# Setup and counting tables in one stage; rescaling and u's first half moved in attention

## The chip, the cores and the metric

The kernel runs on one core of a Trainium2 chip, as one program. Its time is the device time of an execution in microseconds. Engines: PE is TensorE's matmul, PEld its weight load, DVE is VectorE, ACT ScalarE, POOL GpSimd, SP SyncE, which here only issues DMAs. Each engine works through its own queue in order; semaphores order the engines among each other.

## The reference

A graph of N = 3125 nodes with 64 features and E = 103,125 edges, sorted by destination. Four layers, each of the form x = layernorm(x + layer(x)):

```
L0: mean of x[src] over the edges of a dst, two 64x64 products, batch norm, relu
L1: h = x * rsqrt(out_deg[src]); sum over edges * rsqrt(in_deg[dst]); @ W + b
L2: attention over edges. Per edge e, with S = 9 harmonics sh, hidden MLPs wk, wv:
    k[e] = wk[e] * sum_{d,s} x[dst_e,d] * sh[e,s] * Cqk[d,s,:]     (v alike with Cv)
    attn[e,h] = <q[src_e,h], k[e,h]>; softmax over the edges of a node; sum of v * alpha
    @ W_out + x @ W_self, batch norm
L3: messages relu(concat(x[s], x[t]) @ W_msg + b), mean per node, update product, relu
```

The edge list holds each random edge in both directions and one loop per node; the kernel gathers the rows of one end of an edge with an indirect DMA and reaches those of the other by windows of 128 nodes, since dst is sorted.

## The kernel before

Edges are cut into 808 tiles of 128, four tiles to a group of 512 edges: 202 groups. The stages run one behind the other; each is a block of code per engine, and between two blocks all engines meet at a barrier.

**setup** (L98 to L243 of the kernel before). SP (L157) and ACT (L167) issue the loads of all constants and of the edge and node tables, alternately, on one semaphore `loaded`. DVE waits for all of them (ahead of L204), converts dst to float (L204), splits the weight tables Cqk and Cv in a high and a low part (L211 to L216), makes two scaled edge lists (L218 to L221), which SP stores, and `dst_local` and `node_of_part` (L230, L232) from a matmul (L241). POOL fills constants and the identity.

**group_tables** (L253 to L427). The counting stage needs to know which tiles touch which window of 16 nodes. SP loads `tile_last` (L291); POOL writes four iotas (L295 to L301). DVE goes through a chain of some 30 short dependent steps (L351 to L399), with two small matmuls in it (L314, L319), and gets the tile numbers `tile_i`. POOL then gathers the 12 blocks of edge rows with indirect DMAs (L306). DVE waits for all twelve (ahead of L402), computes `lo_f` and `off` from them (to L423), PE transposes both, 12 + 12 (L325, L327), slot by slot, and ACT (L336) and DVE (L427) copy them to `lo_tab` and `key_tab`.

**count_and_sum** (L456 on). DVE first clears the sums (L485), sets the ones in `pieces` (L486) and splits the node rows in three bf16 parts (`split_rows`, L433 to L439). Then for each group of tiles it makes one-hots (L494, L496), PE multiplies them to counts (L538), ACT copies the counts out (L564). Layers 0 and 1 follow.

**attention_loop**. A pipeline over groups g, written out by hand as `body(g)` on each engine; in body g the first work on group g+1 stands beside the last work on group g-1. The order on DVE in one body: z parts 0 and 1 of g+1 (L1547), vx of g-1 (L1576), then in turn low parts 0, 1, 2 (L1553) and z parts 2, 3, 4, low part 3 (L1553), low part 4 (L1556, on partitions 64 to 127 only), u = b_k * wk (L1606), u = b_q * u (L1609), vw (L1612), the pick table of g+2 (L1534), the two scans run (L1583) and top (L1586) that give the running maximum per node, ex (L1591, L1593). ACT makes the high part of each z (L1282), which the low part needs. PE sums u over the heads (L1497), then picks q, sums the previous group by node (L1504, L1507), transposes the gathered rows of the next group (L1423), which ACT copies to `xt` (L1259), and multiplies the z parts with Cqk and Cv (L1450 to L1456).

POOL keeps the sums of all nodes, `acc_den`. Per group it rescales the first column by the factor with which the running maximum moved (L1355), adds the group's four tiles at their windows (L1360), and gathers the rows of a later group, four indirect DMAs (L1341). The rescaling and the adds are one function `add(g)`; it waits for the sums of g and for all five low parts of g+3 (`low_ready`), which DVE makes in body g+2:

```
with pool.Fori(0, G // 2 - 3) as n:
    add(2 * n + 1, 1)
    gather(2 * n + 6, n + 3, 0, False)
    add(2 * n + 2, 0)
    gather(2 * n + 7, n + 3, 1, False)
```

DVE writes `ex` of group g only after the rescaling of g-2 has read it (`added`). The message stage and layer 3 follow attention.

## Time and profile before

| | us |
|---|---|
| median of 3 runs | 5087.5 (5077.75 to 5090.65) |
| profiled execution, its own time | 5084.4 |
| its span, first to last instruction | 5082.7 |
| PE busy | 4378.5 (86%) |
| DVE busy | 4062.3 (80%) |
| ACT busy | 2575.0 (51%) |
| POOL busy | 2381.0 (47%) |

| stretch, us | stage |
|---|---|
| 0 to 34 | setup |
| 34 to 90 | group_tables |
| 90 to 106 | clearing and row split at the head of count_and_sum |
| 106 to 700 | counting |
| 1047 to 3883 | attention |
| from there to 5083 | layer 2's end, messages, layer 3 |

A timeline line gives the start in us, the duration in us, the engine, the line of the kernel, the operation, output <- inputs, and in brackets how long the engine had been idle before it and what released it. SPq, ACTq are DMA issues. Groups of instructions give the number (x), total and mean duration. The granted clock is a fraction of the full one.

### The profile page before, as it was taken

The numbers are of one execution on the slowest core, as the hardware profiler recorded it, in microseconds if no ns is written. First come the engines' busy times: TensorE is split into PE (matmuls) and PEld (weight loads), VectorE is DVE, ScalarE is ACT, GpSimd is POOL, SyncE is SP. The second block draws the span as 40 slices with busy tenths as digits, with TensorE's granted clock in tenths as the row PEclk, the third lists the DMA queues.
The fourth block names the chain that finished last, engine by engine and source line by source line (L and its number), as shares of the span: only waits on it lengthen the run. The fifth ranks groups of instructions, "written<-read, shape, count | busy, mean of one in ns | idle before, by whom it ended". The sixth has DMA issues, their size and how long they took to land. (4 is left out here: it accounts for less than half of the span.)

```text
span 5082.7 us, 93633 instructions
## 1 busy us (share of the span) xinstructions
PE 4378.5 (86%) x21874; PEld 3160.3 (62%) x21874; DVE 4062.3 (80%) x9260; ACT 2575.0 (51%) x5924; POOL 2381.0 (47%) x2660
## 2 busy tenths in 40 slices
PE   1787877879999999999999999999998677777777
PEld 0222343457777777777777777777777566666665
DVE  5999965469999999999999999999994455555554
ACT  0777750047777777777777777777773100000000
POOL 1000000035555555555555555555552477777774
PEclk9999988879999999999999999999997555555555
DMA  2112115378888887888788888788882344444442
GB/s 57 76 76 98 79 51 232 145 165 180 180 180 180 178 180 179 181 179 181 178 179 182 180 180 181 177 181 180 179 181 52 76 100 103 101 103 103 102 103 63
DMA packets 576585, 719.35 MB, mean 142 GB/s; under 512 B 204519, under 2 KB 338727, under 8 KB 572583
## 3 DMA queue, kind: packets, MB, share of 16 engines
q1 hardware_dynamic: 517910, 634.65, 50.5%
q0 software_dynamic: 52288, 81.11, 8.1%
q10 hardware_dynamic: 6288, 2.48, 0.2%
q8 instruction: 38, 0.62, 0.1%
q14 instruction: 61, 0.49, 0.0%
HBM read 663.58 MB, written 54.36 MB: 141 GB/s over the span
## 5 line engine op out<-in xcount | busy, mean ns | idle before, releaser
L1341 POOL DMA_INDIRECT attn_rows<-x_twice,attn_idx x808 | 960.0, 1188 | 237.5 <-issue 203.9
L1696 POOL DMA_INDIRECT msg_rows<-a_rows,msg_idx x808 | 779.0, 964 | 370.2 <-issue 243.6
L1547 DVE TENSOR_TENSOR attn_z<-attn_xt,attn_sh 128x512 f32<-128x512 f32 x1010 | 681.8, 691 | 67.7 <-ACT attn_xt L1259 42.9
L1282 ACT CAST attn_z_hi<-attn_z 128x512 fp32r<-128x512 f32 x1010 | 606.8, 623 | 204.0 <-DVE attn_z L1547 197.6
L1360 POOL TENSOR_TENSOR acc_den<-acc_den,attn_sums 128x256 f32 x808 | 582.7, 721 | 188.7 <-POOL acc_den L1360 151.9
L1734 PE MATMUL msg_at_dst<-msg_bwin,msg_pick 128*128 128x64 f32 x1616 | 397.6, 428 | 271.1 <-DVE msg_pick L1760 218.7
L1734 PEld LDWEIGHTS msg_at_dst<-msg_bwin,msg_pick 128*128 128x128 f32 x1616 | 359.8, 328 | 351.3 <-DVE msg_pick L1760 263.1
L1674 ACT ACTIVATE msg_msg<-msg_pre 128x256 f32<-128x256 f32 x202 | 84.2, 417 | 941.8 <-DVE msg_pre L1775 937.7
L1553 DVE TENSOR_TENSOR attn_z_lo<-attn_z,attn_z_hi 128x512 fp32r<-128x512 f32 x808 | 555.0, 687 | 1.0 <-ACT attn_z_hi L1282 0.8
L1362 POOL MEMSET acc_den<- 128x6656 f32 x1 | 5.6, 5645 | 980.2 <-POOLq L90 980.2
L538 PE MATMUL count_bank<-count_key_hot,count_lo_hot 128*128 128x400 bf16 x1395 | 330.7, 348 | 135.9 <-DVE count_key_hot L496 132.1
L496 DVE TENSOR_SCALAR count_key_hot<-key_iota,key_tab 128x400 bf16<-128x400 f16 x1395 | 429.6, 308 | 0.1
L1355 POOL TENSOR_TENSOR acc_den<-acc_den,attn_ex 128x2 f32 x202 | 38.9, 193 | 822.7 <-DVE attn_z_hi L1556 803.1
L1775 DVE TENSOR_TENSOR msg_pre<-msg_rows,msg_at_dst 128x256 f32<-128x256 f32 x202 | 85.1, 421 | 416.4 <-DMA msg_rows<-a_rows,msg_idx 416.4
L1745 PE MATMUL msg_sums<-msg_onehot,msg_msg 128*64 128x128 f32 x1616 | 397.8, 428 | 2.7 <-ACT msg_msg L1674 2.7
L538 PEld LDWEIGHTS count_bank<-count_key_hot,count_lo_hot 128*128 128x128 bf16 x1395 | 102.9, 100 | 386.9 <-DVE count_key_hot L496 327.2
L1450 PE MATMUL attn_b_v<-attn_z_hi,L_Cv_hi 128*128 128x512 f32 x808 | 340.0, 421 | 0.0
L1450 PE MATMUL attn_b_k<-attn_z_hi,L_Cqk_hi 128*128 128x512 f32 x808 | 335.4, 415 | 0.0
L1745 PEld LDWEIGHTS msg_sums<-msg_onehot,msg_msg 128*64 128x64 f32 x1616 | 317.1, 225 | 26.7 <-ACT msg_msg L1674 3.1
L494 DVE TENSOR_SCALAR count_lo_hot<-lo_iota,lo_tab 128x128 bf16<-128x128 f16 x1395 | 332.8, 239 | 0.0
L1452 PE MATMUL attn_b_k<-attn_z_lo,L_Cqk_hi 128*128 128x512 f32 x808 | 318.4, 394 | 0.0
L1451 PE MATMUL attn_b_v<-attn_z_hi,L_Cv_lo 128*128 128x512 f32 x808 | 317.2, 393 | 0.0
(294 smaller groups left out, 10985.6 us busy)
## 6 DMA issues: line engine op xcount, KB each, us to landing
attn_sh<-in_edge_sh SPq DMA_DIRECT2D x404, 640.0 KB
attn_dst<-dst_scaled SPq DMA_DIRECT2D x202, 256.0 KB
attn_qwin<-q_rows SPq DMA_DIRECT2D x808, 64.0 KB
attn_mask<-dst_step SPq DMA_DIRECT2D x202, 256.0 KB, 3.5
msg_dst<-dst_scaled SPq DMA_DIRECT2D x202, 256.0 KB, 3.2
counts<-chunk SPq DMA_DIRECT2D x15, 3100.0 KB, 9.7
chunk_late<-counts SPq DMA_DIRECT2D x15, 3100.0 KB, 10.3
attn_feat<-in_edge_feat SPq DMA_DIRECT2D x404, 64.0 KB
```

What stands on the lines that cost most here:

```text
L494: nc.vector.tensor_scalar(lo_hot[g % RING][:, s, :], sb["lo_iota"][:], sb["lo_tab"][:, s, g:g + 1], None, ALU.is_equal)
L496: ts = nc.vector.tensor_scalar(key_hot[g % RING][:, s, :], sb["key_iota"][:], sb["key_tab"][:, s, g:g + 1], None, ALU.is_equal)
L538: mm = nc.tensor.matmul(bank[g % 4][:, 0:KEYS], lo_hot[g % RING][:, s, :], key_hot[g % RING][:, s, :], start=(s == 0), stop=(s == SLOTS - 1))
L1282: nc.scalar.copy(z_hi[p][:, c, :], z[:, c % 2, :]).then_inc(high_sb, 1)
L1341: pool.indirect_dma_start(rows[p][:, t, :], None, dram["x_twice"], bass.IndirectOffsetOnAxis(ap=idx[p][:, t:t + 1], axis=0)).then_inc(rows ...
L1360: pool.tensor_tensor(window, window, sums[p][:, :, t, :], ALU.add).then_inc(added, 1)
L1450: nc.tensor.matmul(bank[:], hi[:, c, :], z_hi[p][:, c, :], start=(c == 0), stop=False)
L1547: dve.tensor_tensor(z[:, c % 2, :], xt[p][:], sh[p][:, c, :], ALU.mult).then_inc(z_ready, 1)
L1553: dve.tensor_tensor(z_lo[p][:, c, :], z[:, c % 2, :], z_hi[p][:, c, :].bitcast(F32), ALU.subtract).then_inc(low_ready, 1)
L1696: pool.indirect_dma_start(rows[p][:, t, :], None, dram["a_rows"], bass.IndirectOffsetOnAxis(ap=idx[p][:, t:t + 1], axis=0)).then_inc(rows_ ...
L1734: mm = nc.tensor.matmul(at_dst[p][:, t * D:(t + 1) * D], pick[p][:, t, :], bwin[p][:, t, :], start=True, stop=True)
L1745: mm = nc.tensor.matmul(sums[p][0:D, t, :], msg[p][:, t, :], onehot[p][:, t, :], start=True, stop=True)
```

## The change

setup and group_tables become one block, in place of the latter. `tile_last` is the first load on SP, with a semaphore of its own; the node rows are the first load on ACT, with their own too, and leave the common list, which shifts the alternation of the loads behind them. DVE goes through the tables' chain first; while POOL gathers, it splits the node rows (taken from count_and_sum) and then does the old setup's work; then it waits for the gathers. POOL writes the tables' four iotas first and, behind the constants, clears the sums and sets the ones of `pieces`. PE transposes the lo parts as soon as they are there, the key parts when the old setup's tables have been read out of the same PSUM banks. In attention POOL's rescaling becomes `fade(g)`, issued after `add(g-1)` and ahead of the next gathers; it waits for ex of g and for the top scan of g+1. On DVE low part 4 of the next group moves behind u's first product.

The diff, cut to its core (the chain of L348 to L399 is the same code in the new place):

```diff
         ph = Phase(nc, ctx, "setup")
         loaded = ph.sem("loaded")
         iota_done = ph.sem("iota_done")
+        x_in = ph.sem("x_in")
+        piece_step, pieces_done, cleared = (ph.sem(n) for n in ("piece_step", "pieces_done", "cleared"))
...
+        rest = ph.sb("rest", [P, HB, D])
...
         def _(sp):
+            sp.dma_start(last[:], dram["tile_last"].rearrange("(p k) -> p k", p=P)).then_inc(last_in, 16)
             for to, frm in loads[0::2]:
...
+            act.dma_start(sb["x_rows"][:], dram["x"][0:HB * P, :].rearrange("(h l) d -> l h d", l=P)).then_inc(x_in, 16)
             for to, frm in loads[1::2]:
...
+            act.wait_ge(turned, 1)
+            nc.scalar.copy(sb["win_base"][0:1, :], turn_ps[0:1, 0:GK * P]).then_inc(copied, 1)
+            act.wait_ge(turned, 2)
+            for s in range(SLOTS):
+                nc.scalar.copy(sb["lo_tab"][:, s, :], lo_ps[s][:].rearrange("p k g -> p (k g)")).then_inc(copied, 1)
             act.wait_ge(padded, 64)
...
+            pool.iota(win_iota[:], [[1, NWIN]], base=0, channel_multiplier=0,
+                      allow_small_or_imprecise_dtypes=True).then_inc(ranged, 1)
...
+            pool.memset(sb["acc"][:], 0.0).then_inc(cleared, 1)
+            pool.memset(sb["pieces"][:, :, 2 * D:3 * D], 1.0).then_inc(cleared, 1)
+            pool.wait_ge(sized, 1)
+            for k in range(GK):
+                for s in range(SLOTS):
+                    pool.indirect_dma_start(
+                        edges[:, k, s, :], None, dram["edge_table"],
+                        bass.IndirectOffsetOnAxis(ap=tile_i[:, k, s:s + 1], axis=0)).then_inc(rows_in, 16)
...
+            pe.wait_ge(placed, 1)
+            for k in range(GK):
+                mm = nc.tensor.matmul(turn_ps[0:1, k * P:(k + 1) * P], win_base[:, k:k + 1], sb["ident"][:],
+                                      start=True, stop=True)
+            mm.then_inc(turned, 1)
+            key_flat = [key_ps[k][:].rearrange("p k g -> p (k g)") for k in range(2)]
+            pe.wait_ge(step, 2)
+            pe.wait_ge(dst_float, 1)
+            half = T // 2
+            for k in range(2):
+                mm = nc.tensor.matmul(key_flat[k][:, 0:half], first_row[:], dst_f[:, k * half:(k + 1) * half],
+                                      start=True, stop=True)
+            mm.then_inc(base_bcast, 1)
+            pe.wait_ge(keyed, 1)
+            for s in range(SLOTS):
+                for k in range(GK):
+                    mm = nc.tensor.transpose(lo_ps[s][:, k, :], lo_f[:, k, s, :], sb["ident"][:])
+            mm.then_inc(turned, 1)
+            pe.wait_ge(keyed, 2)
+            pe.wait_ge(tables_done, 5)
+            for s in range(SLOTS):
+                for k in range(GK):
+                    mm = nc.tensor.transpose(key_ps[s][:, k, :], off[:, k, s, :], sb["ident"][:])
+                mm.then_inc(turned, 1)

...
+            dve.tensor_scalar(tile_i[:], tile[:], float(T - 1), None, ALU.min).then_inc(sized, 1)
+            n = 22 + SLOTS
+            dve.wait_ge(x_in, 16)
+            dve.wait_ge(cleared, 2)
+            split_rows(dve, piece_step, sb["pieces"], sb["x_rows"][:], rest[:], 0, pieces_done)
             dve.wait_ge(loaded, 16 * len(loads))
             dve.tensor_copy(dst_f[:], sb["dst_i"][:]).then_inc(dst_float, 1)
...
-                dve.tensor_tensor(sb["dst_local"][:, cols], dst_f[:, cols], base_ps[:, k, 0:half],
+                dve.tensor_tensor(sb["dst_local"][:, cols], dst_f[:, cols], key_flat[k][:, 0:half],
...
-            dve.memset(sb["acc"][:], 0.0).then_inc(cleared, 1)
-            dve.memset(sb["pieces"][:, :, 2 * D:3 * D], 1.0).then_inc(cleared, 1)
-            split_rows(dve, piece_step, sb["pieces"], sb["x_rows"][:], rest[:], 0, pieces_done)
-            dve.wait_ge(cleared, 2)
-
...
-            pe.wait_ge(pieces_done, 1)
...
-            def add(g, p):
-
-                bases = window_bases(nc, mybir.EngineType.Pool, sb, TG * g)
+            def fade(g, p):
+
+                base = nc.values_load_multi_w_load_instructions(
+                    sb["dst_i"][0:1, bass.ds(TG * g, 1)], engines=[mybir.EngineType.Pool], min_val=0, max_val=PADN,
+                    skip_runtime_bounds_check_because="dst holds node numbers below N, and PADN")[1][0]
                 factor = ex[p][:, GE:GE + 1].unsqueeze(1).to_broadcast([P, 2, 1])
-                pool.wait_ge(sum_sb, 2 * (g + 1))
-                pool.wait_ge(low_ready, KC * (min(g + 4, G) if isinstance(g, int) else g + 4))
+                pool.wait_ge(ex_sb, g + 1)
+                pool.wait_ge(topped, min(g + 2, G) if isinstance(g, int) else g + 2)
                 if not is_first(g, 0):
                     pool.wait_ge(added, STEPS * g)
                 pool.sem_inc(pool_go, 1)
-                first_col = sb["acc_den"][:, :, bass.ds(bases[0], 1)]
+                first_col = sb["acc_den"][:, :, bass.ds(base, 1)]
                 pool.tensor_tensor(first_col, first_col, factor, ALU.mult).then_inc(added, 1)
+
+            def add(g, p):
+
+                bases = window_bases(nc, mybir.EngineType.Pool, sb, TG * g)
+                pool.wait_ge(sum_sb, 2 * (g + 1))
+                pool.wait_ge(low_ready, KC * (min(g + 4, G) if isinstance(g, int) else g + 4))
                 for t in range(TG):
                     pool.wait_ge(added, STEPS * g + t + 1)
...
             gather(2, 1, 0, False)
             gather(3, 1, 1, False)
             gather(4, 2, 0, False)
+            fade(0, 0)
             add(0, 0)
+            fade(1, 1)
             gather(5, 2, 1, False)
             with pool.Fori(0, G // 2 - 3) as n:
                 add(2 * n + 1, 1)
+                fade(2 * n + 2, 0)
                 gather(2 * n + 6, n + 3, 0, False)
                 add(2 * n + 2, 0)
+                fade(2 * n + 3, 1)
                 gather(2 * n + 7, n + 3, 1, False)
-            add(G - 5, 1)
-            for g in range(G - 4, G):
+            for g in range(G - 5, G - 1):
                 add(g, g % 2)
+                fade(g + 1, (g + 1) % 2)
+            add(G - 1, 1)

         @block.sync
         def _(sp):
...
                     low(*group, c)
                     make(*group, c + 2)
                 low(*group, KC - 2)
-                low(*group, KC - 1)

             def weigh(g, p):
...
                     dve.wait_ge(k_ps, g + 1)
                     dve.wait_ge(w_sb, 2 * g + 1)
                     dve.tensor_tensor(u[:], b_k[:], wk[:], ALU.mult).then_inc(kw_ready, 1)
+                if next:
+                    low(*after(g, n, p), KC - 1)
+                if front:
                     dve.wait_ge(q_ps, g + 1)
                     dve.wait_ge(kw_ready, g + 1)
                     dve.tensor_tensor(u[:], b_q[:], u[:], ALU.mult).then_inc(u_ready, 1)
...
                 make_pick(g, n, p)
                 split_begin(g, n, p)
                 split_end(g, n, p)
+                low(g, n, p, KC - 1)
                 make_pick(*after(g, n, p))

             dve.wait_ge(dve_set, 4)
...
             early_table("x_rows", [P, HB, D])
             early_table("win_base", [1, GK * P], I32)
             early_table("out_deg", [P, HB])
-            setup(nc, dram, sb)
             early_table("pieces", [P, HB, 4 * D], BF16)
             sb["acc"] = early.enter_context(nc.sbuf_tensor("node_sums", [P, 2, NP], F32))
             with ExitStack() as counting:
@@ -1874,7 +1873,7 @@
                 counting_table("lo_iota", [P, P], FP16)
                 counting_table("key_tab", [P, SLOTS, GK * P])
                 counting_table("lo_tab", [P, SLOTS, GK * P])
-                group_tables(nc, dram, sb)
+                setup(nc, dram, sb)
                 sb["chunk"] = [counting.enter_context(nc.sbuf_tensor(f"chunk{k}", [P, HB, CCOL], FP16))
                                for k in range(KEPT)]
```

## Rows read from the trace of the kernel before

**Rows 1.** Busy time by stretch: stretch, length, each engine's busy us, clock, DMA
```profile
106.00:700.00 594.00, 475.02 (x2090) 172.06 (x2090) 593.38 (x3193) 438.69 (x1164) 0.00 (x0) 0.97 0.18 76
...
2000.00:3000.00 1000.00, 972.34 (x5345) 732.94 (x5344) 952.21 (x1373) 709.14 (x1516) 569.38 (x650) 1.00 0.81 180
```

**Rows 2.** Timeline, 0 to 90 us: start, us, engine, line, operation, idle before
```profile
25.12 0.58 DVE L204 CAST setup_dst_f<-dst_i 128x808 f32<-128x808 int32 x1 [23.77 <-DMA L_W_upd_a<-in_L_W_upd]
...
32.98 0.63 DVE L232 TENSOR_SCALAR node_of_part<-setup_base_ps,iota_col 128x404 f32<-128x404 f32 x1
...
35.98 0.17 DVE L351 TENSOR_SCALAR tables_last<-tables_last 128x7 int32<-128x7 int32 x1 [1.33 <-DMA tables_last<-in_tile_last]
...
51.52 0.17 DVE L399 TENSOR_SCALAR tables_tile_i<-tables_tile 128x12 int32<-128x12 f32 x1
...
65.89 0.95 POOL L306 DMA_INDIRECT tables_edges<-in_edge_table,tables_tile_i  x1 [0.30 <-issue]
70.05 0.96 DVE L402 TENSOR_SCALAR tables_hi_i<-tables_edges 128x1536 int32<-128x1536 int32 x1 [18.36 <-DMA tables_edges<-in_edge_table,tables_tile_i]
...
84.02 1.12 PE L325 MATMUL tables_lo_ps<-ident,tables_lo_f 128*128 128x128 f32 x4 [37.15 <-DVE tables_off L423]
...
89.28 0.69 DVE L427 COPY key_tab<-tables_key_ps 128x512 f32<-128x512 f32 x1 [0.85 <-PE tables_key_ps L327]
```

**Rows 3.** Timeline, 90 to 107 us: the counting stage's entry
```profile
91.72 5.61 DVE L485 MEMSET node_sums<- 128x6656 f32 x1 [1.74 <-issue]
...
98.91 1.76 DVE L433 CAST pieces<-x_rows 128x1600 bf16<-128x1600 f32 x1
...
106.16 0.25 DVE L494 TENSOR_SCALAR count_lo_hot<-lo_iota,lo_tab 128x128 bf16<-128x128 f16 x1
```

**Rows 4.** Timeline, one attention group from 2007 us on
```profile
2007.53 0.69 DVE L1553 TENSOR_TENSOR attn_z_lo<-attn_z,attn_z_hi 128x512 fp32r<-128x512 f32 x1
...
2008.30 0.69 DVE L1556 TENSOR_TENSOR attn_z_hi<-attn_z,attn_z_hi 64x512 fp32r<-64x512 f32 x1
...
2009.02 0.69 DVE L1606 TENSOR_TENSOR attn_u<-attn_b_k,attn_wk 128x512 f32<-128x512 f32 x1
...
2009.33 0.19 POOL L1355 TENSOR_TENSOR acc_den<-acc_den,attn_ex 128x2 f32 x1 [3.55 <-DVE attn_z_hi L1556]
...
2009.82 0.69 DVE L1609 TENSOR_TENSOR attn_u<-attn_b_q,attn_u 128x512 f32<-128x512 f32 x1
...
2010.56 1.13 PE L1497 MATMUL attn_b_attn<-attn_u,head_sum 128*128 128x512 f32 x2 [0.36 <-DVE attn_u L1609]
2010.68 0.73 POOL L1360 TENSOR_TENSOR acc_den<-acc_den,attn_sums 128x256 f32 x1 [0.25 <-POOL acc_den L1360]
...
2011.02 0.93 DVE L1534 TENSOR_TENSOR attn_pick<-attn_dst,node_of_part 128x512 f32<-128x512 f32 x1
...
2012.79 0.72 POOL L1360 TENSOR_TENSOR acc_den<-acc_den,attn_sums 128x256 f32 x1 [0.25 <-POOL acc_den L1360]
2013.18 1.41 DVE L1586 TENSOR_TENSOR_SCAN attn_top<-attn_mask,attn_run 128x512 f32<-128x512 f32 x1
...
2013.66 1.70 POOL L1341 DMA_INDIRECT attn_rows<-x_twice,attn_idx  x1
...
2014.84 0.59 ACT L1259 COPY attn_xt<-attn_b_xt 128x512 f32<-128x512 f32 x1 [1.61 <-PE attn_b_xt L1423]
...
2015.56 1.29 DVE L1547 TENSOR_TENSOR attn_z<-attn_xt,attn_sh 128x512 f32<-128x512 f32 x2
```

**Rows 5.** Waits, 2000 to 3000 us: us in total, times, longest
```profile
PE attn_b_attn L1497 <- DVE attn_u L1609: 26.2, 72, 0.4
```

**Rows 6.** Single lines: duration ns min/median/max, first and last start
```profile
L1606 DVE TENSOR_TENSOR attn_u<-attn_b_k,attn_wk x202: 690/692/694, 1080.4 to 3862.2; 128x512 f32<-128x512 f32 x101
...
L1534 DVE TENSOR_TENSOR attn_pick<-attn_dst,node_of_part x202: 679/841/945, 1050.6 to 3839.7; 128x512 f32<-128x512 f32 x101
```

**Rows 7.** The page's groups: busy us, mean ns, idle before
```profile
L1341 POOL DMA_INDIRECT attn_rows<-x_twice,attn_idx x808 | 960.0, 1188 | 237.5 <-issue 203.9
```

More of the change, by code:

```diff
@@ L425, in _ @@
             for s in range(SLOTS):
[L426 removed]
+                dve.wait_ge(turned, s + 3)
                 dve.tensor_copy(sb["key_tab"][:, s, :], key_ps[s][:].rearrange("p k g -> p (k g)")).then_inc(copied, 1)
[L430 to L439 removed]
 LOADED = 8
```

312 lines of the change are left out of this document (130 added, 182 removed).

## The prediction

> **What bounds the kernel now.** I read the busy time by stretch first, then the timeline of the first 107 us, then the timeline of one attention group with the waits of its stage. They show three things.
>
> The counting stage is VectorE's: in 106 to 700 us DVE is busy 593.38 of 594.00 us [rows 1]. Whatever lies before its first one-hot moves the rest of the program by its full length. What lies before it is a chain with long holes. DVE waits until 25.12 us for the constant loads, works until 33.6, crosses a barrier, starts the tables at 35.98, hands the tile numbers over at 51.69, then waits 18.36 us for twelve gathers, works until 89.97 and crosses another barrier [rows 2]. From 91.72 to 106.16 it clears the sums and splits the node rows; only then does the first one-hot start [rows 3].
>
> Attention runs 202 groups. The first product of u starts at 1080.4 in the first and at 3862.2 us in the last [rows 6], so a group takes 2781.8/201 = 13.84 us. In 2000 to 3000 us PE is busy 97.2% and DVE 95.2% [rows 1]. Both are in the loop. PE waits for u before the head-sum matmul, 26.2 us in 72 groups or 0.36 us each [rows 5]; after it PE runs without a hole to the transposes of the next rows, ACT copies them (14.84 to 15.43) and DVE's next z starts at 15.56 [rows 4]. DVE gets there by its own work (pick, two scans, ex) at the same moment. So from u's end to the next z two paths of equal length lie side by side, and from z to u's end there is one path, DVE's. A group gets shorter only between z and u, and by 0.36 us at most: then PE has no hole left.
>
> **The merged stage.** With the last window's tile numbers loaded first on SP, I redo the chain.
> - Tile numbers: DVE stood idle 1.33 us for this small load [rows 2]; with the two memsets ahead of that wait I count 1.6 us. Issued at about 0.8, it lets DVE begin at 2.5. It now competes with the node rows on the other queue; I allow 0.5 more: 3.0. GpSimd's four iotas come first on its queue and need a microsecond, as before.
> - Chain to the tile numbers: 51.69 - 35.98 = 15.7 us [rows 2]: 18.7.
> - The twelve gathers: 18.4 us from there to DVE's next step [rows 2]: 37.1.
> - Into that hole go the row split, 106.16 - 98.91 = 7.25 us [rows 3], until 26.0, and the old setup's DVE work, 33.61 - 25.12 = 8.5 us [rows 2], until 34.5. The loads landed at 25.1 before; they are the same loads less one, so they are there at 26.0. Cover is left for 2.6 us; beyond that each microsecond of late loads counts in full.
> - After the gathers: 89.97 - 70.05 = 19.9 us [rows 2]. TensorE's 24 transposes ran in order lo, key, slot by slot, behind the last VectorE step (84.02 to the last copy's start at 89.28). The twelve lo ones now run earlier, beside VectorE, so half of the 5.26 us goes: 17.3. Stage end at 54.4.
> - Clearing (91.72 to 98.91, 7.2 us [rows 3]) goes to GpSimd, which is idle between its constants and the gathers. If its memsets are about as long as VectorE's they end near 12 us, well before 18.7. ScalarE's copy of the window bases sits behind its DMA issues until 25 us and is wanted only in the counting stage. A fill of the queues costs nothing here, since nothing but the loads waits for it.
> - Barrier and entry: 91.72 - 89.97 = 1.75 us: first one-hot at 56.2 instead of 106.16. That is 50.0 us less.
>
> Two costs are not in the rows of this stretch. GpSimd now clears while VectorE runs its table chain, and VectorE now works while GpSimd generates gathers. Nearest rows: a pick that overlaps GpSimd's adds takes 0.93 us instead of 0.68 [rows 4, 6], which on the some 7 us of clearing would be 2.6 us; and gathers in attention take 1.188 us in the mean [rows 7] against 0.95 for the undisturbed one of the tables [rows 2], 12 x 0.24 = 2.9 us. Below stands zero, and no reason for a gain. I take 5.0 of these 5.5 us, because the gathers share their whole length with VectorE work. The front gives 45 us, with 51 and 38 as ends (38: the costs double, and the loads come 1 us too late).
>
> The Trainium skill (SBUF — State Buffer, section Who interferes with whom) says that GpSimd and VectorE share a port pair as an exclusive lock: VectorE's copies and tensor-scalar instructions in a 2-port mode wait for any GpSimd instruction to end, those with two SBUF inputs only for one that reads SBUF. By that rule a tensor-scalar of the chain could stand behind the whole 5.6 us memset, and the gathers' descriptor writes behind the conversions of the old setup; the front would then give about 42 instead of 50 us. No row here shows a 2-port instruction beside a GpSimd memset.
>
> **u's first half before the last low part.** The order was low 3, low 4, u1, u2; it becomes low 3, u1, low 4, u2. Starts of today [rows 4]: 2007.53, 2008.30, 2009.02, 2009.82: the steps are 0.77 + 0.72 + 0.80 = 2.29 us, the last because u2 reads what u1 has just written. Two instructions that don't wait start about 0.60 apart (u2 at 9.82, two steps to pick at 11.02 [rows 4]). Upper end of the gain: three steps of 0.60, 0.49 us. Lower end by rows: the steps around low 4, which works on partitions 64 to 127 only, are both long and stay 0.72; only low 3 to u1 becomes 0.60, so 2.04 us and a gain of 0.25. u2's inputs are early enough (wk and the product of k were ready long before; ScalarE's last high part ends at about 8.27, and low 4 now starts at 8.85). I take 0.25, the value nearest to a row that shows low 4's own neighbours.
>
> The Trainium skill (VectorE: DVE Perf Modes, section Two Vector instructions with no wait between them) says that an instruction whose first SBUF input starts in another quadrant of partitions than the one before is held until that has finished. By that, low 4 is held and so is what follows it, and the gain is 0.25; without the rule it could be 0.49, cut to 0.36 by PE.
>
> **GpSimd's rescaling.** It moves from before the adds of its group to after the adds of the group before, and waits for the top scan. Today it starts 0.34 us behind low 4's end (2008.99 to 2009.33), and the adds follow: the second starts at 2010.68, idle 0.25 us after a first of the same 0.73, which so started at 2009.70 [rows 4]. Now the first add stands in its place, 0.34 us behind low 4; low 4 ends 0.55 us later, so the first add comes at 9.88 instead of 9.70. What it waits for: the top scan ends at 2014.59, and the four gathers, which started at 2013.66 [rows 4], are queued behind it. They start about 1.2 us later. GpSimd's day: four gathers of 1.19 us in the mean [rows 7] and the gaps, some 6 us, until about 2020.9, next adds not before 2023.4; today it idles 3.55 us there [rows 4]. The rows are read two bodies later (started 2013.66, used at about 2028), with over 6 us left. So this costs nothing at these places.
>
> Where adds and VectorE's two SBUF-to-SBUF instructions meet matters more. Pick starts at 11.02, 0.34 behind the second add, and takes 0.93; top takes 1.41 beside the last add. With u2's end 0.25 earlier and the first add 0.18 later, the second add would start at 10.77 to 10.86 and pick at 10.77. Who comes first is open. If pick does, VectorE wins up to 0.3 us that PE's path hides; if the add does, pick and top end where they end today, and the 0.25 is gone. Bounds: gain 0.36 (PE full), loss 0.14 (pick and top each held by most of an add, 0.39 us more than with pick first, less the 0.25). I take 0.22 a group: 0.25, less a little for groups in which the add comes first. Times 202: 45 us.
>
> **Sum.** The profiled execution took 5084.4 us (span 5082.7), the median of the runs is 3.1 above it. 5084.4 - 45 - 45 = 4994.4; on the median's level 4997.5.
>
> **Rivals.**
> - A, the adds eat it: the shifted adds meet pick and top in each group, the period stays 13.84 and only the front counts: 5087.5 - 45 = 5042. For it: pick's excess of 0.25 us today comes from the add in front of it, and top lies beside the last add. Against it: pick's start moves to the add's start or ahead of it.
> - B, PE full: steps of 0.60 around low 4 too, 0.36 a group: 5087.5 - 45 - 73 = 4970.
> - C, the front is dearer: the chain stands behind GpSimd's memsets, or the loads land after 28.6 us. Ten us less than I take: 5007.
> - D, slower: the gathers, held until the top scan is over, now start exactly beside the next group's z's instead of beside the scan. Today's first gather takes 1.70 us against 0.95 undisturbed [rows 4, 2]. If VectorE has to bear that 0.76 us, z starts late, z is on the single path, and a group grows by 0.76 - 0.25 = 0.51 us: +103 us, less 45: 5146. It decides from 0.47 us a group (45/202 + 0.25) on. Against it: the three later gathers run beside the z's today, and the first two z's still take only 1.29 us together [rows 4].
> - That the change does not do what it says: the stage would have to wait for the loads ahead of the tables. The order in the code excludes it, since the chain waits for its own semaphore.
>
> **How the numbers follow.** The likeliest case 0.55 (own range 4983 to 5015), A 0.17, B 0.14, C 0.10, D 0.04. The range goes from B to A with their own spread, 4965 to 5044. Within 0.3% (15 us) no difference can be told from none. All cases but D are faster by over that; between A and D a little lies inside: faster 0.94, same 0.02, slower 0.04.
>
> **What would show it.** First one-hot at 56 to 61 us; no hole before the tables; DVE's wait for the gathers cut from 18.4 to 2 to 7 us; clearing on GpSimd before the gathers. In attention: u's two halves with low 4 between them, starts 0.60, 0.72 and 0.72 apart; PE's wait for u at 0.1 us instead of 0.36; the period at 13.6. A period of 13.84 with pick at 0.93 or more is A; a PE without the wait and 13.5 is B. The prediction is wrong if the first one-hot comes after 68 us, or if the period does not move.

## The result, and the profile after

The changed kernel takes 5045.7 us (median of 4, 5041.8 to 5048.1) against 5088.6 us (median of 4) for the kernel before beside it: ratio 0.992 [0.9908, 0.9931], 42.9 us less. Forecast was 4997 with a range down to 4965 and up to 5044; the time lies 49 us above the forecast and just above the range. That is the place of rival A (front gained, attention not: 5042), though not by A's mechanism. The profiled execution took 5048.1 us, its span is 5046.4. A few executions fall in a slower state (one of the kernel before took 6257 us beside 5078); all medians here are over the others.

The front first. Timeline of the changed kernel, 0 to 64 us (start, us, engine, line, operation, idle before), to be laid beside [rows 2, 3]:

```profile
2.58 0.45 DVE L321 TENSOR_SCALAR setup_last<-setup_last 128x7 int32<-128x7 int32 x1 [1.08 <-DMA setup_last<-in_tile_last]
...
5.08 5.64 POOL L261 MEMSET node_sums<- 128x6656 f32 x1
...
7.21 4.99 DVE L334 TENSOR_SCALAR setup_need_i<-setup_need 128x196 int32<-128x196 f32 x1
...
10.66 1.43 POOL L262 MEMSET pieces<- 128x1600 bf16 x1
...
12.24 0.26 DVE L336 TENSOR_SCALAR setup_need_i<-setup_need_i 128x196 int32<-128x196 int32 x1
...
23.27 0.17 DVE L369 TENSOR_SCALAR setup_tile_i<-setup_tile 128x12 int32<-128x12 f32 x1
23.34 1.81 DVE L103 CAST pieces<-x_rows 128x1600 bf16<-128x1600 f32 x1
23.73 1.10 POOL L266 DMA_INDIRECT setup_edges<-in_edge_table,setup_tile_i  x1 [11.64 <-DVE setup_tile_i L369]
...
39.90 0.95 POOL L266 DMA_INDIRECT setup_edges<-in_edge_table,setup_tile_i  x1 [0.30 <-issue]
45.09 0.96 DVE L406 TENSOR_SCALAR setup_hi_i<-setup_edges 128x1536 int32<-128x1536 int32 x1 [5.49 <-DMA setup_edges<-in_edge_table,setup_tile_i]
...
61.93 0.69 DVE L431 COPY key_tab<-setup_key_ps 128x512 f32<-128x512 f32 x1 [0.16 <-PE setup_key_ps L300]
62.94 0.25 DVE L479 TENSOR_SCALAR count_lo_hot<-lo_iota,lo_tab 128x128 bf16<-128x128 f16 x1 [0.32 <-PEq L114]
```

The first one-hot starts at 62.94 in place of 106.16 us: 43.2 us, forecast 45. VectorE waits 5.49 us for the gathers instead of 18.36. One line stands out: L334 and L336 have the same size, but L334 took 4.99 us, to within 0.1 us of the end of GpSimd's second memset (10.66 + 1.43 = 12.09).

Now attention. Single line, busy time in 2000 to 3000 us (stretch, length, each engine's busy us, clock, DMA), and the waits of that stretch (us in all, times, longest), of the changed kernel:

```profile
L1602 DVE TENSOR_TENSOR attn_u<-attn_b_k,attn_wk x202: 680/683/692, 1036.0 to 3826.3; 128x512 f32<-128x512 f32 x101
```

```profile
2000.00:3000.00 1000.00, 978.28 (x5331) 731.88 (x5330) 934.44 (x1369) 708.57 (x1514) 592.37 (x649) 1.00 0.78 179
```

```profile
DVE attn_z L1544 <- ACT attn_xt L1243: 36.7, 63, 1.6
...
PE attn_b_xt L1420 <- DMA attn_rows<-x_twice,attn_idx: 10.9, 26, 1.1
```

A group takes (3826.3 - 1036.0)/201 = 13.88 us against 13.84 [rows 6]. The first group's u starts 44.4 us sooner than before (1036.0 against 1080.4), the last group's only 35.8 (3826.3 against 3862.2): the front gives its part, and attention gives nothing and takes some 8 us back. PE's wait for u (0.36 us a group, [rows 5]) has gone from the list. In its place PE waits for the gathered rows, 10.9 us in 26 of 72 groups, and VectorE's z waits for ScalarE's copy of them, 36.7 us. The wait for u is gone and the group is not shorter: something else now ends last. Timeline of the changed kernel, one such group and the start of the next, beside [rows 4]:

```profile
2052.56 0.68 DVE L1602 TENSOR_TENSOR attn_u<-attn_b_k,attn_wk 128x512 f32<-128x512 f32 x1
...
2053.27 0.69 DVE L1553 TENSOR_TENSOR attn_z_hi<-attn_z,attn_z_hi 64x512 fp32r<-64x512 f32 x1
...
2053.99 0.69 DVE L1608 TENSOR_TENSOR attn_u<-attn_b_q,attn_u 128x512 f32<-128x512 f32 x1
...
2055.19 1.19 POOL L1352 TENSOR_TENSOR acc_den<-acc_den,attn_sums 128x256 f32 x1 [0.25 <-POOL acc_den L1352]
2055.20 0.68 DVE L1531 TENSOR_TENSOR attn_pick<-attn_dst,node_of_part 128x512 f32<-128x512 f32 x1
...
2057.22 1.22 DVE L1582 TENSOR_TENSOR_SCAN attn_top<-attn_mask,attn_run 128x512 f32<-128x512 f32 x1
...
2057.51 1.44 POOL L1352 TENSOR_TENSOR acc_den<-acc_den,attn_sums 128x256 f32 x1 [0.25 <-POOL acc_den L1352]
...
2059.21 0.19 POOL L1341 TENSOR_TENSOR acc_den<-acc_den,attn_ex 128x2 f32 x1 [0.25 <-POOL acc_den L1352]
...
2059.36 0.65 PE L1420 MATMUL attn_b_xt<-ident,attn_rows 128*128 128x128 f32 x4 [0.82 <-DMA attn_rows<-x_twice,attn_idx]
...
2060.04 0.96 POOL L1325 DMA_INDIRECT attn_rows<-x_twice,attn_idx  x1 [0.64 <-PE attn_b_xt L1420]
2060.05 0.59 ACT L1243 COPY attn_xt<-attn_b_xt 128x512 f32<-128x512 f32 x1 [2.39 <-PE attn_b_xt L1420]
...
2060.76 1.29 DVE L1544 TENSOR_TENSOR attn_z<-attn_xt,attn_sh 128x512 f32<-128x512 f32 x2 [1.36 <-ACT attn_xt L1243]
...
2067.20 0.68 DVE L1602 TENSOR_TENSOR attn_u<-attn_b_k,attn_wk 128x512 f32<-128x512 f32 x1
...
2080.78 0.68 DVE L1602 TENSOR_TENSOR attn_u<-attn_b_k,attn_wk 128x512 f32<-128x512 f32 x1
```

What the reader is to see: u's part is as forecast (0.71 and 0.72 us between the starts). This group lasts 2067.20 - 2052.56 = 14.64 us, the next 13.58. The difference is the wait for the rows: z starts 6.77 us behind u's second half (2060.76 - 2053.99), 5.74 where rows are in time [rows 4]. The gathers start 6.05 us behind u's second half; in [rows 4] that is 2013.66 - 2009.82 = 3.84. Over groups 20 to 190 the means are 6.05 and 3.69 us.

### The profile page after: what moved, and what is told of

Same layout as the page of the kernel before. It is cut to its first block and busy times, and to the rows that moved or that the text cites. A ratio compares the mean times of both kernels' runs of the same rounds, so it can differ in the third digit from the quotient of the medians.

```text
span 5046.4 us, 94426 instructions
## 1 busy us (share of the span) xinstructions
PE 4396.7 (87%) x21874; PEld 3157.3 (63%) x21874; DVE 4011.2 (79%) x9258; ACT 2577.4 (51%) x5924; POOL 2467.9 (49%) x2662
## 5 line engine op out<-in xcount | busy, mean ns | idle before, releaser
L1352 POOL TENSOR_TENSOR acc_den<-acc_den,attn_sums 128x256 f32 x808 | 760.9, 942 | 754.7 <-DVE attn_z_hi L1553 592.4
L1325 POOL DMA_INDIRECT attn_rows<-x_twice,attn_idx x808 | 856.7, 1060 | 330.4 <-issue 277.4
L1448 PE MATMUL attn_b_k<-attn_z_hi,L_Cqk_lo 128*128 128x512 f32 x808 | 316.4, 392 | 0.0
```

What stands on the lines that cost most here:

```text
L1325: pool.indirect_dma_start(rows[p][:, t, :], None, dram["x_twice"], bass.IndirectOffsetOnAxis(ap=idx[p][:, t:t + 1], axis=0)).then_inc(rows ...
L1352: pool.tensor_tensor(window, window, sums[p][:, :, t, :], ALU.add).then_inc(added, 1)
L1448: nc.tensor.matmul(bank[:], lo[:, c, :], z_hi[p][:, c, :], start=False, stop=False)
```

## The experiments

Theory T: u's move gives its 0.25 us a group, and late rows take it back, because the gathers start late and their rows land after PE wants them. The rivals: A (the adds eat u's gain: an add and a VectorE instruction that meet are stretched; the expectations call it L, the lock), M (the transfers' rate is the bound, not their start), F (the rescale's new place is dear by itself).

Four sets of four kernels ran, each set on one chip with the kernel before beside it. The chips are of two kinds: in sets 2 and 4 the kernel before takes 5078 and 5076 us, in sets 1 and 3 it takes 5395 and 5380. Ratios hold within a set. G is the mean start of the gathers, in us behind the start of u's second half; in the expectations that is "u2 + ...".

| set | kernel | median, us | ratio [interval] | period, us | G, us |
|---|---|---|---|---|---|
| 1 | front_only | 5347.9 | 0.9897 [0.9878, 0.9916] | 13.84 | 3.69 |
| 1 | u_only | 5478.4 | 1.0154 [1.0132, 1.0175] | 14.45 | 5.16 |
| 1 | fade_only | 5410.6 | 1.0037 [1.0016, 1.0058] | 14.18 | 5.68 |
| 1 | rows_early | 5298.6 | 0.9815 [0.9797, 0.9833] | 13.56 | a group ahead |
| 2 | after_again | 5040.4 | 0.9928 [0.9911, 0.9946] | 13.89 | 6.05 |
| 2 | u_only_again | 5004.0 | 0.9850 [0.9827, 0.9872] | 13.68 | 5.17 |
| 2 | gather_first | 5006.3 | 0.9862 [0.9843, 0.9882] | 13.73 | 4.69 |
| 2 | best | 4988.3 | 0.9830 [0.9811, 0.9848] | 13.57 | a group ahead |
| 3 | fade_only_again | 5454.9 | 1.0136 [1.0107, 1.0165] | 14.47 | 5.70 |
| 3 | front_only_again | 5333.2 | 0.9912 [0.9895, 0.9930] | 13.84 | 3.69 |
| 3 | old_u_early | 5320.8 | 0.9884 [0.9864, 0.9904] | 13.81 | a group ahead |
| 3 | best2 | 5265.8 | 0.9785 [0.9768, 0.9803] | 13.56 | a group ahead |
| 4 | after_third | 5039.6 | 0.9927 [0.9910, 0.9944] | 13.89 | 6.05 |
| 4 | fade_only_third | 5046.1 | 0.9944 [0.9927, 0.9960] | 13.92 | 5.68 |
| 4 | u_mid | 5054.5 | 0.9960 [0.9946, 0.9974] | 13.94 | 6.80 |
| 4 | u_late | 5071.3 | 0.9991 [0.9981, 1.0000] | 14.05 | 7.73 |

### The front alone: front_only, front_only_again

Both of attention's moves are undone (the order of `low` and u on VectorE, rescale and adds in one function on GpSimd).

> The merged stage alone; attention exactly as before the change (rescaling ahead of its own adds, low part 4 ahead of u's first product). Theory T (rows land too late for TensorE since the gathers start later; the u step works) and theory L (the shifted adds lock VectorE's pick and top scan) both expect the period of 13.84 us and the front's 43 us in full: 5044 to 5047 us, no rows late. Theory M (the transfers can't keep up with less than about 13.9 us a group, whatever the order) expects the same.

> The merged front alone, both of attention's moves undone. It measured 0.9897 on another chip. First one-hot at 62.5 to 63.5 us where the kernel before has it at 106.2, attention's period 13.84 to 13.86 as before, time 41 to 46 us below before: ratio 0.9910 to 0.9920. More than that would say that the front gives something to a later stage.

Ratios 0.9897 and 0.9912, period 13.84 as before. By the medians both are 47 us under the kernel before; in the second the first one-hot starts at 63.22 us, 43 sooner. The interval of the second, 38 to 56 us, holds the 43; that of the first, 45 to 66, starts just above it. So the front gives what its timeline says, and whether it gives a few us more to later stages stays open.

### Each move alone: u_only, fade_only and their repeats

```
u_only:    the changed kernel, but on GpSimd
-   add(2n+1); fade(2n+2); gather(2n+6)
+   fade(2n+1), add(2n+1) as one function; gather(2n+6)
fade_only: the changed kernel, but on VectorE
+   low(*group, KC - 1)            # ahead of both halves of u again
-   low(*after(g, n, p), KC - 1)   # between them
```

> Merged stage and u's first product ahead of low part 4, but GpSimd's rescaling back ahead of its own adds. T: the first add comes 0.37 us later than in the changed kernel, the gathers no longer stand behind the rescaling; they start some 5.2 to 5.4 us after the start of u's second product instead of 6.05, so about half of the lateness goes: period 13.65 to 13.80, 5000 to 5030 us. L: pick or top is held more often, period 13.85 or more, 5045 or more. M: 13.88, 5045.

> Merged stage and the moved rescaling, but low part 4 ahead of u's first product as before. T: low part 4 and the adds come 0.5 us earlier to u, so the gathers start about 5 us after u's second product; the group is 13.84 anyway without lateness and rows are late rarely: 13.84 to 13.90, 5044 to 5055 us. L: pick held as before, 13.84. M: 13.88.

> The front and u's move, GpSimd's order of before, a second time. It measured 1.0154 of the kernel before, with a period of 14.45 us, where theory T expected 13.65 to 13.80 us (its rows were in time). If ScalarE's idle time ahead of L1260 and L1282 (26.8 and 15.9 us in 72 groups) is a property of this kernel's code, it is there again: period 14.4 to 14.5, ratio 1.012 to 1.018. If it belongs to the chip, it shows in the changed kernel of this set as well, or in neither: then this one has a period of 13.65 to 13.80 and a ratio of about 0.988.

> The front and GpSimd's rescale moved ahead of its turn, u's move undone. Theory T: u costs its 0.22 us a group again, and the gathers start at u2 + 5.7 in place of + 3.7, 8.1 us or less before their use; period 13.85 to 14.0 us, ratio to the kernel before 0.991 to 0.996. With the other three corners (before's order of both 0.99, u's move alone 0.985, both 0.9928) this gives what the rescale's move costs: theory T puts it at 0 to 0.1 us a group without u's move and 0.21 with it, as only with u's move the group is short enough for the rows to end last. Rival F (the rescale's move is dear by itself, whatever u does): 0.2 us a group here too, period 14.05, ratio 0.998.

> GpSimd's move alone, u's undone. Where before takes 5080 us: theory T has the rows in time for the longer group of 13.85 us (8.1 us or more from last issue to use against 6.4 to 7.3 for the landing): period 13.85 to 13.95, ratio 0.991 to 0.995; rival F: 14.05, ratio 0.998 or more. Where before takes 5380 us it measured 1.0037 and 1.0136, with ScalarE's idle time of 10 and 35 us in 72 groups, and is expected there again.

Set 1 missed by far, for both: u_only (period 14.45, expected 13.65 to 13.80) and fade_only (14.18, expected 13.84 to 13.90) are slower than before. On this chip u_only's rows are nearly in time (PE waits 2.3 us in 6 of 72 groups), and instead ScalarE stands idle with nothing that the trace can name ("remote"). Waits of u_only, set 1, 2000 to 3000 us:

```profile
DVE attn_z_lo L1537 <- ACT attn_z_hi L1266: 50.0, 48, 1.7
...
ACT attn_hid L1260 <- remote: 26.8, 19, 1.8
...
ACT attn_wk L1282 <- remote: 15.9, 21, 1.0
```

In set 2 the same kernel has none of these lines, takes 13.68 us a group and 0.985 of before: this is where T had put it. Waits of u_only_again:

```profile
DVE attn_z L1531 <- ACT attn_xt L1243: 25.4, 73, 1.2
PE attn_b_xt L1407 <- DMA attn_rows<-x_twice,attn_idx: 3.3, 8, 0.6
```

So the idle time belongs to the pair of kernel and chip. It is back in fade_only_again, on the other slower chip (34.8 us in 29 cases ahead of L1282, period 14.47, a miss for theory T and for rival F), and absent in fade_only_third. On the chips where the changed kernel was timed it does not occur, so sets 2 and 4 are read for the rest. There, u's move alone takes 36 us less than both moves together. Rival A falls with it: in u_only_again the adds lie beside pick and top as well (first add 0.68 us behind u's second half, second, third and fourth near 1.6, 2.7 and 3.7, the fourth up to 1.5 us long), and the gain is there. The rescale's move alone gives 0.9944 and a period of 13.92, as T expected (13.85 to 13.95) and F did not (14.05).

### The gathers alone, earlier or later: gather_first, u_mid, u_late, after_again, after_third

```
gather_first:  add(2n+1); gather(2n+6); fade(2n+2)      # was add, fade, gather
u_mid:   u_only, and in gather:  pool.wait_ge(xt_sb, g)
u_late:  u_only, and in gather:  pool.wait_ge(z_ready, KC * (g - 1) + 1)
```

> The changed kernel with GpSimd issuing a group's gathers ahead of the next group's rescale in place of behind it: they start about 0.6 us earlier (u2 + 5.4 in place of + 6.05), which is a quarter of what the change delayed them by. Theory T: PE's wait for the rows falls from about 11 us in 72 groups to under 4, the period from 13.88 to about 13.65, time 35 to 50 us under the changed kernel's. Rival M (the period is held by the transfers' own rate, not by when they start): period and wait as in the changed kernel, within 0.05 us. If the rescale now falls into DVE's lock or delays the next adds, adds 1 and 2 show it, and the period stays above 13.75.

> u's move alone (front and u moved, GpSimd's order of before), and in the loop each group's gathers wait besides for ScalarE's copy of the previous group's rows (xt_sb), so that they start at u2 + 5.8 us in place of + 5.2; nothing else is changed. Points so far on one chip: start at + 4.7 period 13.73, + 5.2 period 13.69, + 6.05 (the changed kernel) 13.91. Theory T (only the start counts): period 13.75 to 13.90, and PE's wait for the rows between 3 us and 11 us in 72 groups; on a chip where u's move alone is at 0.985, a ratio of 0.987 to 0.992. Rival F (the rescale's own place costs, not the start): period 13.69 and the time of u's move alone.

> The same with the gathers waiting for VectorE's first product of the previous group (z_ready), which ends at u2 + 6.4: they start 1.2 to 1.3 us later than in u's move alone and 0.4 later than in the changed kernel. Theory T: the slack between landing and use, 0.97 us on average in the changed kernel with a floor near 0.6, is gone in every group; each 0.1 us later then costs 0.1: period 14.0 to 14.3, PE's wait for the rows 20 us or more in 72 groups, ratio 0.995 to 1.01, slower than the changed kernel. Rival F: period 13.69.

> The changed kernel as it stands, run beside the others of this set, so that they have it on their own chip. Theory T (rows land late in attention, which costs about 0.3 us a group): period of the attention groups 13.85 to 13.95 us where the transfers are as quick as in its first profile, with PE's wait for attn_rows at about 11 us in 72 groups; ratio to the kernel before 0.990 to 0.994. Rival S (what cost u's move alone 0.6 us a group, ScalarE standing idle ahead of L1260 and L1282 with no event of the kernel to end it, belongs to the chip it ran on and not to the code): the same idle time shows here too, 20 to 40 us in 72 groups, period 14.2 or more, ratio 1.00 or above.

> The changed kernel beside these, on their chip. Where before takes 5080 us: 0.991 to 0.994, period 13.9. Where before takes 5380 us or more, ScalarE stood idle ahead of L1282 with no event of the kernel to end it, in the kernels with one of the two moves (16 to 35 us in 72 groups) and in none with neither move or with rows early: if that comes from the gathers falling later into the group, it is here too, 15 us or more, and the ratio is above 1.00; if not, 0.991 to 0.994 as on the other chip.

In u_mid and u_late the rescale stands where it stood before the change; only the gathers wait longer. The period goes from 13.68 to 13.94 and 14.05, the time from 0.985 to 0.996 and 0.9991. That is the gain of u's move and in u_late the front's too, lost by later gathers alone. Waits of u_late, then one late group of it:

```profile
POOL attn_rows L1327 <- DVE attn_z L1533: 192.0, 72, 3.8
...
PE attn_b_xt L1409 <- DMA attn_rows<-x_twice,attn_idx: 25.5, 36, 1.8
```

```profile
2041.81 1.24 POOL L1327 DMA_INDIRECT attn_rows<-x_twice,attn_idx  x1 [2.10 <-DVE attn_z L1533]
...
2045.99 1.02 POOL L1327 DMA_INDIRECT attn_rows<-x_twice,attn_idx  x1 [0.30 <-issue]
...
2053.98 0.66 PE L1409 MATMUL attn_b_xt<-ident,attn_rows 128*128 128x128 f32 x4 [1.29 <-DMA attn_rows<-x_twice,attn_idx]
```

The last of four gathers ends its issue at 2047.01; PE gets the rows at 2053.98, 6.97 us later. Half of the groups are late (36 of 72), not every one as I had expected, since a late group gives the next one more room: in places groups of about 15 and of 13.57 us alternate (14.98, 13.57, 15.08, 13.57). The gathers start later than I expected, in u_mid at + 6.80, not + 5.8, and in u_late at + 7.73, not about + 6.4: a late copy delays the next gathers too. Rival F predicted 13.69 for both and falls. gather_first has the same start within half a us as u_only_again and the same time; it was expected 35 to 50 us under the changed kernel and is 34 (its start came 1.4 us earlier, not 0.6: in a little under half of the groups the gathers start at + 4, in the others at + 5.2).

Taken as one series, G against the period: 4.69 and 13.73, 5.17 and 13.68, 6.05 and 13.89, 6.80 and 13.94, 7.73 and 14.05. Above 5.2 us a further us of delay costs 0.07 to 0.24 us a group. Below it the mean start says nothing more, but the rows are still late in some groups: with the rows a group ahead (next section) the period is 13.56, 0.12 less than in u_only_again.

Where the lost time lies can be read off the start of VectorE's first z behind u's second half (means over groups 20 to 190; "over" is the period above 13.56):

| kernel | first z, us | behind 5.74 | period over |
|---|---|---|---|
| rows_early, best | 5.74 | 0 | 0 |
| u_only_again | 5.84 | 0.10 | 0.12 |
| gather_first | 5.86 | 0.12 | 0.16 |
| the changed kernel | 6.03 | 0.29 | 0.32 |
| u_mid | 6.12 | 0.38 | 0.37 |
| u_late | 6.24 | 0.50 | 0.49 |

All have u's new order. The z, late by ScalarE's copy of the rows, accounts for nearly the whole of each difference. PE's own wait (10.9 us in 72 groups of the changed kernel, 0.15 each) shows only half of it. fade_only_third, with u's old order, has its first z at 5.81 and 0.08 us a group over front_only: that small cost is late rows too. In u_only on the slower chip z starts at 5.84 as in u_only_again, so the idle time of ScalarE that makes its group 0.77 us longer lies behind z.

### The rows one group ahead: rows_early, old_u_early

```
 add(2n+1); fade(2n+2)
-gather(2n+6)
+gather(2n+7)            # prologue one gather longer, tail one shorter
```

> The changed kernel with each gather issued one group earlier in GpSimd's queue (in the same place of the group, for the next group's rows), so that rows have some 13 us more to land. Nothing else is changed: adds, rescaling and VectorE's order stay. T: no rows are late any more, the period falls to 13.57 to 13.63, 202 groups x 0.27 = 55 us less than the changed kernel: 4985 to 4995 us. L: nothing of the loss was the rows', it stays at 13.88 and 5046. M: the same bytes per group, so it stays at 13.88 with another transfer late (harmonics or query windows).

> The front and the rows one group earlier, u's move undone: tells whether u's move is worth its 0.22 us a group once no row is late, or whether the early rows alone give the whole of it. Theory T: in the kernel before and in the front alone no row was late (0.3 us in 1 of 72 groups), so early rows give nothing there: PE's wait for u back at 26 us in 72 groups, period 13.80 to 13.86, ratio 0.990 to 0.992. Rival E (early rows free attention by themselves, by spreading the transfers): period 13.65 or less, ratio under 0.987.

Single lines of rows_early and old_u_early (first halves of u):

```profile
L1605 DVE TENSOR_TENSOR attn_u<-attn_b_k,attn_wk x202: 681/684/693, 1035.7 to 3761.7; 128x512 f32<-128x512 f32 x101
```

```profile
L1606 DVE TENSOR_TENSOR attn_u<-attn_b_k,attn_wk x202: 691/692/693, 1036.3 to 3812.8; 128x512 f32<-128x512 f32 x101
```

With the changed order of both engines kept and only the rows asked for a group sooner, the group takes (3761.7 - 1035.7)/201 = 13.56 us: 0.28 less than before and 0.32 less than in the changed kernel. Both periods are as theory T expected them (rows_early by 0.01 us below its range). No line of its waits has the rows any more. GpSimd's gathers stand no earlier within a group than in the changed kernel (6.57 us behind u's second half, there 6.05); so neither the lock nor the mere presence of the gathers beside the z's held it (rivals A, D, and M, as the same bytes now move in less time). Without u's move the early rows give only 0.03 us (13.81), and PE's wait for u is at 26.1 us again: u's move is what makes the gain (0.25 us a group), the rows are what let it through. old_u_early also has the rescale in its new place and is no slower than before for it, which is a second answer to rival F.

### The front's lock: best, best2

```
-pool.memset(acc), pool.memset(pieces)       # ahead of GpSimd's wait for tile_i
+dve.memset(acc), dve.memset(pieces)         # best: ahead of the row split
+pool.memset(acc), pool.memset(pieces)       # best2: behind the 12 gathers
```

Both have rows_early's order in attention.

> The changed kernel with the attention's rows gathered one group earlier, and with the two memsets of acc and pieces on VectorE ahead of its wait for x_rows in place of GpSimd's. Theory T with the lock (L334 stood behind GpSimd's two memsets, 4.99 us where its kind takes 0.26): L334 back to about 0.3 us, the first one-hot at 58 to 60 us where the changed kernel has it at 62.9, attention's period 13.56 us, time 3 to 5 us below that of the kernel with the rows early alone (0.9815 of before): 0.980 to 0.982. Rival (the 4.99 us were not the memsets): L334 still 4 us or more, and the time of the rows-early kernel.

> The changed kernel with the rows one group earlier, and GpSimd's two memsets behind its 12 gathers in place of ahead of its wait for their addresses. L334 at 0.26 us, as with the memsets on VectorE; but VectorE, which there was filled from 18.6 to 57 us by 7 us of memsets, now stands free for the gathers' landing at 40 to 41 us unless GpSimd's memset of acc (5.6 us from about 36.7) holds its last operations on the loads back. If it does not: first one-hot at 58.4 to 59.0 us. If it does, VectorE is late by up to 4 us and the one-hot comes at 60 to 62.5. Attention's period 13.57, time within 3 us of that with the memsets on VectorE (ratio 0.981 to 0.984).

Timeline of best, 7 to 61 us, and of best2:

```profile
7.23 0.26 DVE L332 TENSOR_SCALAR setup_need_i<-setup_need 128x196 int32<-128x196 f32 x1
...
18.56 0.17 DVE L367 TENSOR_SCALAR setup_tile_i<-setup_tile 128x12 int32<-128x12 f32 x1
20.06 5.61 DVE L369 MEMSET node_sums<- 128x6656 f32 x1 [1.33 <-issue]
...
42.60 0.63 DVE L402 TENSOR_SCALAR node_of_part<-setup_key_ps,iota_col 128x404 f32<-128x404 f32 x1
43.15 0.95 DVE L405 TENSOR_SCALAR setup_hi_i<-setup_edges 128x1536 int32<-128x1536 int32 x1
...
60.99 0.25 DVE L478 TENSOR_SCALAR count_lo_hot<-lo_iota,lo_tab 128x128 bf16<-128x128 f16 x1 [0.32 <-PEq L114]
```

```profile
7.48 0.26 DVE L334 TENSOR_SCALAR setup_need_i<-setup_need 128x196 int32<-128x196 f32 x1
...
36.59 5.66 POOL L267 MEMSET node_sums<- 128x6656 f32 x1
...
41.21 3.23 DVE L405 TENSOR_SCALAR setup_hi_i<-setup_edges 128x1536 int32<-128x1536 int32 x1 [6.50 <-DMA setup_edges<-in_edge_table,setup_tile_i]
```

The 4.99 us were GpSimd's memsets: with them gone the instruction takes 0.26, and the tile numbers are there 4.7 us sooner. Of these only 2.3 reach the first one-hot (60.99 against 63.29 in after_again; I had expected 58 to 60, a miss), because VectorE now carries 7 us of memsets and no longer waits for the gathers at all: L405 follows L402 at once. In best2 the memset meets L405 behind the gathers, 3.23 us in place of 0.95, and the one-hot starts at 61.31. The lock moves, it does not go. best is the fastest measured on the chips of the first kind: 4988.3 us, 52 under the changed kernel of its set (ratio 0.983, expected 0.980 to 0.982, no difference that its interval shows); best2 has the lowest ratio, 0.9785 (expected 0.981 to 0.984, a miss), but on another chip, and the two were not compared on one.

## Why the prediction was wrong

**The front** was right in its sum and off in two terms that cancel in part: the lock on the chain was dearer by 2.1 us than the 2.6 allowed for it, the entry cheaper by 1.4. Forecast 56.2 with nothing added, 61 with the 5 us that I allowed; measured 62.9. The chain to the tile numbers took 20.7 us from L321's start (2.58 to 23.27), not 15.7: the excess is L334's 4.7 us. I had spread 2.6 us over it as for pick. The Trainium skill (SBUF — State Buffer, section Who interferes with whom) has a VectorE tensor-scalar in a 2-port mode wait for the whole of a GpSimd instruction that was issued first. Here the trace agrees, 4.99 us against 0.26, and the front's 43.2 us lie near the 42 that the prediction worked out by this rule and did not take. The gathers took 21.65 us to L406 (23.44 to 45.09), forecast 18.4 and 2.9 for the overlap. Behind them 17.5 us against 17.3. The barrier's entry took 0.32 us, forecast 1.75: VectorE no longer clears there.

**u's move** was right. The steps are 0.71 and 0.72 as its rows said, PE's wait is gone, and with rows in time a group takes 13.56 or 13.57: 0.25 us less than the same kernel with u's old order (13.81), against a forecast of 0.22 (times 202 that is 44.4 us, which the prediction gives as 45). The Trainium skill (VectorE: DVE Perf Modes, section Two Vector instructions with no wait between them) has low 4 and its follower held; the starts 0.71 and 0.72 us apart agree, where two instructions that are not held start 0.60 apart.

**The order with pick** was settled as hoped: in the group shown pick comes 0.01 us behind the second add, takes 0.68 instead of 0.93, and the add takes 1.19 instead of 0.73. GpSimd pays. I counted this as costing nothing, since GpSimd idles.

**The step that failed** is "They start about 1.2 us later. [...] The rows are read two bodies later (started 2013.66, used at about 2028), with over 6 us left. So this costs nothing at these places." Both halves are wrong. The delay was mis-sized, and the time from the last issue to the rows' landing was put at nothing; with 6 us left the delay would not have mattered.
- The delay behind u's second half is 2.36 us (6.05 less 3.69). 0.25 of it is u itself, which comes earlier; counted as I forecast, it is 2.1 us, not 1.2. I had let the gathers start with the end of the top scan. What ends last is the fourth add: it meets the scan and takes 1.44 us, so that it lasts to + 4.96 where the scan ends at + 4.45. Then comes the rescale at + 5.22, and the first gather another 0.64 behind its end. On average 1.31 us of the delay are the adds' later end and 1.05 the rescale with its gaps. u's move alone, without the rescale's, already delays the gathers by 1.48 us (5.17 less 3.69). Every loss of the lock that I had put on GpSimd's idle time came out at its last instruction, and that was a gather.
- There were not 6 us left but 2.4 before the change, and less than that after it. By the packets of the gathers' queue, the last row of a group lands 6.40 us (mean; 8.29 at most) after the last gather's issue, and PE uses them 8.84 us after it: 2.44 us left on average, 0.75 at the least. The prediction's "over 6 us" comes out if the gathers' issue (to about 2020.9) is subtracted from their use at 2028 and nothing for the landing: 7.1 us. The landing under attention's own traffic takes 6.40 of them. In the tables the rows were there some 3 us behind the last issue [rows 2] (65.89 + 0.95 to 70.05), and I had no row for the landing beside 180 GB/s of other transfers [rows 1].
- The shorter group takes its part as well: u's gain is also 0.25 us less for the rows. In the changed kernel (after_again) the landing takes 6.35 us, the use comes 7.32 us after the issue, and 0.97 are left on average. That is no slack: in 98 of 170 groups PE starts later than u's end alone would let it (over 4.45 us behind u's second half, 4.39 with the rows early), and in these it starts 0.6 to 1.1 us after the last row has landed, 0.85 in the median. No group has less than 0.6.

**Rival D** had the right sentence, that the gathers come later and this lies on the way to z, with a wrong mechanism (a longer first z) and size: z still takes 1.29 us for two. It was weighed by whether VectorE suffers from the gathers, never by whether the rows are late. Rival A had the right time (5042) by chance.

**What was missing** was a rival with late rows. With the rows in time the forecast's sum holds: rows_early is 49 us under front_only in its set, and forecast for attention was 45; its ratio, 0.9815, would be 4994 us beside the result's 5088.6 (an estimate, as it ran on another chip), and the forecast was 4997.

What stays open: what ends ScalarE's idle time ahead of L1260 and L1282 on the slower chips, in kernels with one of the two moves, and whether the changed kernel has it there. It was not run on such a chip. Open too is what sets the 6.4 us of landing: no run changed the other transfers.

## What to carry to other kernels

When a stretch of an engine is called idle, look at what is queued at its end. Time lost to a lock or to a moved step there comes out at the next DMA issue, and the transfer's own path (issue of all parts, landing under load, the time from landing to the reader's start) has to fit before its use; measure that from last issue to use, not from first issue. A prefetch that can be asked for one iteration earlier at the same place takes the question away; here it cost nothing (13.81 us a group in old_u_early, 13.84 without). And a gain that shortens an iteration also takes its length off the slack of every transfer in flight.

## What the runs showed of the hardware

- Landing of four 64 KB gathers beside 180 GB/s of other transfers: 5.9 to 6.8 us from the end of the last issue on average where the gathers of a group do not wait for anything, 4.9 and 5.7 in u_late and u_mid, and up to 8.3 in single groups. Their issue takes 4.9 to 5.7 us. In the tables of the kernel before, with 28 GB/s in the stretch, VectorE got the last of 12 gathered blocks 3.2 us after its issue.
- A VectorE tensor-scalar that meets a running GpSimd memset takes 4.99 or 3.23 us in place of 0.26 or 0.95. In the changed kernel the second GpSimd add, which starts 0.01 us ahead of VectorE's pick, is the one held: 1.19 us in the group shown, 1.12 on average, where the first add takes 0.69.
- Chips differ by 6%: the kernel before takes 5395 and 5380 us on two, 5076 to 5089 on others. In u_only, on one of the slower, the message stage moves 75 to 82 GB/s, in after_third, on one of the others, 101 to 104. A small edit (u_only) had 0.985 on one chip and 1.0154 on another, so a ratio of one chip isn't a verdict for all.
